# Perceiver layer on one core: where the value products and the slot work stand among the score steps, and one Newton iteration for both halves

## The reference

```
x = x + xattn(layernorm(x), ctx)      # 16 heads of 16, softmax over 4096 context rows
x = x + attn(layernorm(x))            # causal linear attention
x = x + ffn(layernorm(x))             # silu(x wg) * (x wu), then wd; 768 hidden columns

# attn: each q and k row is first divided by its norm
xn = x / jnp.maximum(jnp.linalg.norm(x, axis=-1, keepdims=True), 1e-12)
feat = jnp.exp(clip(einsum(xn, omega) * sqrt_2s - s)) / sqrt(M) ...
```

## Time and profile before

| | |
|---|---|
| median of 3 runs | 915.33 us |
| the profiled execution | 914.84 us, of which 913.1 us lie between its first and last instruction |
| granted TensorE clock, mean | 0.979 |
| TensorE busy | 844.7 us, 93% |
| ScalarE busy | 532.0 us, 58% |
| VectorE busy | 432.7 us, 47% |
| first scores of batches 0, 1, 2, 3 | 41.57, 207.38, 413.26, 619.43 us |
| end of the last values | 816.8 us |

### The profile page before, as it was taken

One profiled execution on the slowest core, in us unless ns is written; L12 is line 12 of the kernel. 1 busy time (PEld: TensorE's weight loads), 2 busy tenths in 40 slices (PEclk: granted clock), 3 DMA queues, 4 the chain that ended last, 5 costly groups with the idle time before them and its releaser, 6 DMA issues.

```text
span 913.1 us, 20640 instructions
## 1 busy us (share of the span) xinstructions
PE 844.7 (93%) x8815; PEld 573.3 (63%) x8815; DVE 432.7 (47%) x796; ACT 532.0 (58%) x578; POOL 48.3 (5%) x76
## 2 busy tenths in 40 slices
PE   6799999999999999999899999999999999978776
PEld 4566666666566666666566666666566666646555
DVE  6532235355744446535744446534744445214653
ACT  2167777676577666656577666657577666840101
POOL 1033000000000000000000000000000000000000
PEclk9899999999999999999999999999999999998799
DMA  5757564465333333336343333336334333001000
GB/s 178 236 182 246 207 206 163 147 202 174 127 140 139 139 139 133 107 135 183 128 139 139 139 140 114 116 136 191 117 139 140 139 117 116 1 24 24 1 1 15
DMA packets 58738, 120.09 MB, mean 132 GB/s; under 512 B 21521, under 2 KB 29713, under 8 KB 55121
## 3 DMA queue, kind: packets, MB, share of 16 engines
q1 hardware_dynamic: 56848, 114.31, 36.8%
q0 software_dynamic: 1792, 4.40, 1.6%
HBM read 78.84 MB, written 37.75 MB: 128 GB/s over the span
## 4 chain that ended last, share of the span: by engine, by line
PE 75%; DVE 10%; issue 6%; ACT 4%; DVEq 2%; DMA 1%; POOL 1%; SPq 0%; POOLq 0%; ACTq 0%
PE ps_o L750 23%; PE ps_s L762 16%; PE ps_pa L594 10%; PE ps_pa L555 10%; ACT probs L1026 3%; PE ps_pa L720 2%; PE ps_pa L695 2%; PE ps_pa L707 2%; PE ps_pa L686 1%; PE ps_pa L616 1%; PE ps_pa L643 1%; PE ps_pa L699 1%; DVE feat L1264 1%; DVE feat L1248 1%; DVE ss L1250 1%
## 5 line engine op out<-in xcount | busy, mean ns | idle before, releaser
L1026 ACT ACTIVATE probs<-ps_s 128x1024 f32<-128x1024 f32 x512 | 495.9, 1023 | 272.0 <-PE ps_s L762 243.1
L750 PE MATMUL ps_o<-probs,values 128*17 128x256 f32 x4096 | 258.1, 382 | 0.0
L762 PEld LDWEIGHTS ps_s<-qstack,kstack 64*128 64x128 f32 x2048 | 139.9, 185 | 116.9 <-issue 57.4
L762 PE MATMUL ps_s<-qstack,kstack 64*128 64x256 f32 x2048 | 196.8, 307 | 13.1 <-ACT probs L1026 12.2
L750 PEld LDWEIGHTS ps_o<-probs,values 128*17 128x17 f32 x4096 | 101.4, 97 | 99.4 <-issue 14.3
L1063 DVE TENSOR_SCALAR kparts<-ps_pa,b_heads 128x512 fp32r<-128x512 f32 x64 | 48.0, 751 | 123.8 <-PE ps_pa L555 123.8
L1080 DVE TENSOR_TENSOR values<-ps_pa,bv_pair 128x512 f32<-128x512 f32 x64 | 44.3, 692 | 109.6 <-PE ps_pa L594 109.3
L594 PE MATMUL ps_pa<-wv_hi,ctx_hi 128*128 128x256 f32 x256 | 78.3, 306 | 1.6 <-DVE wv_lo L1051 1.6
L594 PE MATMUL ps_pa<-wv_hi,ctx_lo 128*128 128x256 f32 x256 | 72.5, 283 | 0.0
L594 PE MATMUL ps_pa<-wv_lo,ctx_hi 128*128 128x256 f32 x256 | 72.5, 283 | 0.0
L555 PE MATMUL ps_pa<-ctx_hi,wk_hi 128*128 128x512 f32 x128 | 57.7, 451 | 4.5 <-DVE kparts L1065 2.3
(11 more groups left out here) (238 smaller groups left out, 798.1 us busy)
## 6 DMA issues: line engine op xcount, KB each, us to landing
kstack<-kscr SPq DMA_DIRECT2D x96, 512.0 KB, 5.3
...
qstack<-qscr SPq DMA_DIRECT2D x12, 256.0 KB, 3.7
...
xh<-x SPq DMA_DIRECT2D x4, 256.0 KB, 6.4
...
qstack<-ksample SPq DMA_DIRECT2D x4, 256.0 KB, 4.0
```

The source lines that it names most:

```text
L750: last = mm(ps_o[32 * j:32 * j + DH + 1, g * S:(g + 1) * S], values[par][:, i, head_of_step(g, j), :], prob[:, j * S:(j + 1) * S], start=b ...
L762: last = mm(ps_s[s % 2][:, j * S:(j + 1) * S], kstack[par][rows, u, i * P:(i + 1) * P], queries[rows, u, :], start=True, stop=True)
L1026: nc.scalar.activation(probs[n % AHEAD][:, :], ps_s[n % 2][:, :], ACT.Exp, scale=float(DH) ** -0.5).then_inc(fast["exp_done"], 1)
```

## The change

1. Quads that hold no wide stage, and all quads of batch 0, now run as: scores 0 and 1, the values of the four steps of the quad before, scores 2 and 3, and then all four slots. Quads with a wide stage keep their order. 2. `ss0` only squares and sums; `ss1` takes floor and Newton steps for both halves in one go, on 64 columns. 3. `gu0`, `gate4`, `gu5`, `gate5`, `down` and the head stages behind `ln0` move by 1 to 6 steps (so the queries `q` of the next head stand in the quad of `gu4`, ahead of its key projection, and `max0` in the quad of `gu5`); ScalarE takes a gate's tanh and copy behind the last exponential of its quad where the quad has no wide stage. 4. The warm matmuls in front of tail stages are counted anew, with 14 ahead of `A0` and 12 ahead of the wait for the verdict. 5. SyncE stores the output after the second key half instead of ahead of it.

```diff
@@ -75,18 +75,20 @@
       "norm0": 24, "norm1": 25, "qkT0": 25, "qkT1": 28,
       "feat0": 32, "feat1": 38, "A0": 42, "A1": 46, "feat2": 48, "pv0": 50, "A2": 54, "A3": 58, "pv1": 60, "feat3": 62,
       "A4": 64, "A5": 70, "pv2": 72, "A6": 74, "A7": 78, "pv3": 82, "o2T0": 84, "o2T1": 85, "y2T": 88, "wout": 89,
-      "ln2T": 94, "gu0": 97, "gate0": 98, "gu1": 99, "gate1": 100, "gu2": 101, "gate2": 104, "gu3": 105, "gate3": 108,
-      "gu4": 109, "gate4": 110, "gu5": 112, "gate5": 113, "down": 118}
+      "ln2T": 94, "gu0": 96, "gate0": 98, "gu1": 99, "gate1": 100, "gu2": 101, "gate2": 104, "gu3": 105, "gate3": 108,
+      "gu4": 109, "gate4": 112, "gu5": 115, "gate5": 116, "down": 124}
 TAIL = list(AT)
-HEAD_AT = {"ln0": 86, "ln0T": 102, "q": 106, "kbd": 110, "max0": 114, "max1": 115, "max2": 116, "max3": 117,
-           "maxT": 120}
-WARM = {"yT": 18, "ln1T": 10, "qkT0": 32, "y2T": 3, "ln2T": 10, "gu0": 3, "down": 5}
+HEAD_AT = {"ln0": 86, "ln0T": 104, "q": 108, "kbd": 110, "max0": 112, "max1": 116, "max2": 117, "max3": 120,
+           "maxT": 121}
+WARM = {"yT": 30, "ln1T": 14, "qkT0": 22, "A0": 14, "y2T": 3, "ln2T": 12, "gu0": 3, "down": 5}
+WARM_JUDGED = 12
 NORMALISED = TAIL.index("oT1") + 1
 FEATS = [f"feat{f}" for f in range(G)]
 WIDE = FEATS + [f"A{p}" for p in range(H // 2)]
 GATES = [f"gu{k}" for k in range(HB)]
 
-ACT_BEHIND = {**{n: 1 - AT[n] % 2 for n in FEATS}, **{n: 1 - AT[n] % 2 for n in GATES}}
+WIDE_QUADS = {AT[n] // QUAD for n in WIDE}
+ACT_BEHIND = {n: 1 - AT[n] % 2 if AT[n] // QUAD in WIDE_QUADS else QUAD - 1 - AT[n] % QUAD for n in FEATS + GATES}
 
 NEEDS = {"maxT": "max3", "oT0": "o", "oT1": "o", "qk1": "ln1T", "v": "ln1T", "qkT0": "norm0", "qkT1": "norm1",
          **{n: "qkT1" for n in FEATS}, **{f"A{p}": "qkT1" for p in range(H // 2)},
@@ -476,8 +478,6 @@
                         load_head(fast, b + 1, (fast["product"], fast.at("product", head_of(b), "ln0T")))
                     if q + 2 < B * NCH:
                         write_key_half(fast, q + 2, p % 2, 0)
-                    if b and p == AT["down"] // STEPS:
-                        store(fast, tail_of(b - 1), b - 1)
                     if b + 1 < B and p == HEAD_AT["q"] // STEPS:
                         write_queries(fast, head_of(b + 1))
                         stack_queries(fast, b + 1, qstacks[(b + 1) % 2])
@@ -485,6 +485,8 @@
                         shift_queries(fast, head_of(b + 1), qstacks[(b + 1) % 2])
                     if q + 2 < B * NCH:
                         write_key_half(fast, q + 2, p % 2, 1)
+                    if b and p == AT["down"] // STEPS:
+                        store(fast, tail_of(b - 1), b - 1)
             load_x(fast, B - 1, (fast["operand"], fast.at("operand", tail_of(B - 2), "down")))
             write_output(fast, tail_of(B - 1))
             regroup_output(fast, B - 1)
@@ -796,6 +798,14 @@
                     pe.wait_ge(fast["operand"], fast.at("operand", tail_of(b - 1), "o"))
                 value_product(fast, n, s, q % 2, q % NCH == 0, q % NCH == NCH - 1, q * TT + s // G)
 
+            valued = [0]
+
+            def values_up_to(n):
+
+                while valued[0] < n:
+                    fast_values(valued[0])
+                    valued[0] += 1
+
             def fast_slot(b, p, s):
 
                 q = b * NCH + p
@@ -840,25 +850,25 @@
                     pe.wait_ge(fast["k_stacked"][p % 2], (q // 2 + 1) * STACKED)
                     for s in range(0, STEPS, QUAD):
                         n = q * STEPS + s
-                        halves = s == 0 or any(name in WIDE for t in range(QUAD)
-                                               for name, _ in stages_at(b, p * STEPS + s + t))
-                        for t in (0, 1):
-                            fast_scores(b, q, s + t)
-                        for t in (0, 1):
-                            fast_slot(b, p, s + t)
-                        if halves and n:
+                        if b and (p * STEPS + s) // QUAD in WIDE_QUADS:
+                            for half in (0, 2):
+                                for t in (0, 1):
+                                    fast_scores(b, q, s + half + t)
+                                for t in (0, 1):
+                                    fast_slot(b, p, s + half + t)
+                                values_up_to(n + half)
+                        else:
                             for t in (0, 1):
-                                fast_values(n - LAG + t)
-                        for t in (2, 3):
-                            fast_scores(b, q, s + t)
-                        for t in (2, 3):
-                            fast_slot(b, p, s + t)
-                        for t in range(LAG if halves else 0, QUAD):
-                            fast_values(n - LAG + t)
-            for t in range(LAG):
-                fast_values(B * BS + t - LAG)
+                                fast_scores(b, q, s + t)
+                            values_up_to(n)
+                            for t in (2, 3):
+                                fast_scores(b, q, s + t)
+                            for t in range(QUAD):
+                                fast_slot(b, p, s + t)
+            values_up_to(B * BS)
             products(fast, TAIL[:NORMALISED], tail_of(B - 1), True)
 
+            warm(ps_p, WARM_JUDGED)
             pe.wait_ge(judged, 1)
             nc.tensor.transpose(ps_a[0:1, 0:P], den_ok[:, 0:1], ident[:, :]).then_inc(judged, 1)
             products(fast, TAIL[NORMALISED:], tail_of(B - 1), True)
@@ -1247,11 +1257,13 @@
                     sq = feat[:, 0, n, :, :].rearrange("p c s -> p (c s)")
                     v.tensor_tensor(sq, qk[:, n, :], qk[:, n, :], ALU.mult)
                     dve.drain()
-                    v.tensor_reduce(ss[:, n, :], sq.rearrange("p (h d) -> p h d", d=DH), AX.X, ALU.add)
-                    dve.drain()
-                    v.tensor_scalar(ss[:, n, :], ss[:, n, :], 1e-24, None, ALU.max)
-                    dve.drain()
-                    last = inverse_root(rnorm[:, n, :], ss[:, n, :], sq[:, 0:2 * H])
+                    last = v.tensor_reduce(ss[:, n, :], sq.rearrange("p (h d) -> p h d", d=DH), AX.X, ALU.add)
+                    if n == ST - 1:
+                        every, roots = (a[:, :, :].rearrange("p t h -> p (t h)") for a in (ss, rnorm))
+                        dve.drain()
+                        v.tensor_scalar(every, every, 1e-24, None, ALU.max)
+                        dve.drain()
+                        last = inverse_root(roots, every, sq[:, 0:ST * 2 * H])
                 elif kind == "norm":
 
                     qk3 = qk[:, n, :].rearrange("p (h d) -> p h d", d=DH)
```

## The result

The changed kernel takes 903.11 us, the median of four runs (900.96, 901.60, 904.62, 911.17), beside 915.39 for the kernel before on the same chip. The ratio is 0.9879, 95% interval 0.9836 to 0.9922. The forecast was 900.5 with a range of 894 to 908: the time lies in it, 2.6 above the forecast. A second series of six runs on another occasion gave 907.07, ratio 0.9903 (0.9867 to 0.9938).

What follows compares the result with a forecast made beforehand. TensorE, busy 93% of the span, was taken to bound the kernel with its waits. Loop gains 19.4 less costs 10.5 give 9; 914.84 - 9 - 2.6 (tail Newton) - 3.0 (tail clock) = 900.2, forecast 900.5, range 894 to 908.

Steps and rivals of the forecast that it cites:

- One sign that the prediction itself named for being wrong: Loop: a batch of 206 us that has not lost 1 to 2 us would show the prediction wrong.
- The last step of the forecast: Whole kernel: 900.2 for the profiled execution, plus 0.5 for the median of the runs, given as 900.5.
- Ordinary and first quads: Loop: ordinary quads keep 4.83 us; batch 0's chunk starts, 5.58 before, come to 4.83 too, 0.75 less each.
- the slower rival: Plain quads: ScalarE's release by values of n-4 comes 0.94 late, 0.7 lost in each of 92, 965 us; chance 0.04.
- the terms of the sum for batch 0: Batch 0: seven chunk starts gain 0.75 each; a delayed value projection costs 0.35, `maxT` and `max0` about 1.4.
- The added waits: Loop: VectorE work now in the open before `feat0`, `qk0`, `gu4`, `gu5`, `gu1` and in batch 0 costs 10.5 us.
- the claim of the gains that `oT1` only stops waiting: Loop, `oT1`: its bank waits, 0.8 us in all over three batches, go.
- Newton in the loop: Batches 1 to 3: joint Newton leaves VectorE ahead of `qk1`, so `qkT0` comes 0.7 earlier in each, 2.1 us.
- The end of batch 3: Last quad of batch 3: `down`'s 5.4 us of matmuls cover exponentials that stood in the open, about 1.6 us gained.
- Tail, Newton: Tail: joint Newton shortens a VectorE chain TensorE waits for, 2.6 us; 22 warm matmuls for 32 stay inside the wait.
- Tail, clock: Tail: fourteen warm matmuls ahead of `A0` fill 3.2 of 3.78 us idle and keep the clock at full, 3.0 us gained.
- The rule against Newton: Loop and tail: optimizing the busiest engine first would make Newton at VectorE's 47% worth nothing, the sum 4.7 us less; term kept.

Runs made afterwards that it cites:

- after_again: The changed kernel run once more with nothing altered, as the measure for the runs beside it: 907.07 us, ratio 0.990 to the kernel before.
- order_alone: Kernel before with only the new order inside quads and new places of tanh and features; old step numbers, warm matmuls and Newton: 926.43 us, ratio 1.012.

## Why the prediction was right, and where not

The time came out where it was forecast, but the sum that gave it did not hold term by term. The loop gave 5.8 of the 9 us, and 1.6 of these are the clock of the profiled execution of the kernel before. One sign that the prediction itself named for being wrong came true: batches 1 and 2 were to lose 1 to 2 us of their 206, and batch 2 takes 206.9 us, before 206.2, in `after_again` 205.6 (batch 1 204.4 both times, before 205.9). The last step of the forecast has a slip too: 900.2 and 0.5 are 900.7.

**Ordinary and first quads.** Right. 4.85 against the 4.83 forecast; no score waits for ScalarE in a plain quad, so the slower rival, a release one exponential late, did not come. Batch 0 is 5.6 shorter, of which 3.1 belong to the order; the terms of the sum for batch 0 give 3.5.

**The added waits.** Right in place and nearly in size. `feat0` 1.18 of added time in each of three batches (1.05 forecast), `qk0` 0.57 (0.6), `gu4` 0.98 (0.7), `gu5` 0.72 (0.7), `gu1` 0.38 (0.35). The next batch's first scores after batch 0 wait 1.36 for `maxT`'s transfer (1.4). `max0` in batch 0 costs 0.8 and not 0.15.

**The missed wait.** The sum has no term for the output's transfers. The step that failed is the claim of the gains that `oT1` only stops waiting, 0.8 us to the good. The quads at step 4 do lose 0.14, 0.13 and 0.48. But `oT1` also moved to the end of its quad, and its two writes leave 1.6 to 1.9 us later. That alone costs nothing, since `yT`'s turn moved by as much, as batch 1 shows. In batches 2 and 3 the second write also takes 2.2 and 1.2 us longer, and `yT` waits 1.8 and 0.8, 2.8 in all from start to start. Why it takes longer is open, so following the stages and their transfers through the new order would have found the place, but not the size.

**Newton in the loop.** At its place, steps 24 to 27, the forecast was 2.1 us and the three quads are 1.3 shorter, but not for its reason. `order_alone`, with the old Newton, has them 2.3 shorter: it is the new order that takes the wait away, and joint Newton gives 1.0 of it back. By itself it is worth 1.3 in the old order. The step that failed is the reading of the earlier trace rows: it set the new instruction stream into the old order's idle times. The two edits meet on VectorE.

**The end of batch 3.** Forecast 1.6 from `down` as cover for the last exponentials. From step 96 on the piece is 0.2 shorter while it holds two steps of values more, so on equal work it gave 1.2; with its other terms (two cuts gone, `gu1`) the sum has 1.5. ScalarE's pace did stand in the open, and stands there less now. The waits of TensorE for it from step 96 of batch 3 on, before and after:

```profile
PE ps_s L762 <- ACT probs L1026: 4.2, 9, 0.9
```

```profile
PE ps_s L764 <- ACT probs L1036: 3.3, 7, 0.9
```

So this term was right in its mechanism and somewhat too large.

Of the 9 us forecast for the loop the missed wait takes 2.8 and Newton 0.8, which leaves 5.4. The clock at the start of the kernel before adds 1.6. Measured are 5.8, so the other terms together fell 1.2 short: among them 0.6 at step 0 of batches 1 to 3 (0.77, 0.46 and 0.47 for 0.75 each), 0.4 at `feat0`, 0.6 at `gu4` and 0.4 in batch 0, against gains that the runs don't split.

**Tail, Newton.** 2.59 measured for 2.6 forecast, but as 1.69 from Newton and 0.90 from the warm count. The sentence that 22 warm matmuls for 32 are "still inside the wait" is true; that 32 would be so too, and the count therefore worth nothing, isn't.

**Tail, clock.** The profiled execution has the 3 us (`A0` to `y2T` 21.6 for 23.9, `qkT0` to `A0` 7.3 for 8.2). The size holds, and with the fourteen matmuls the clock is at full at `A0` as forecast, but the gain is not shown to be theirs: three executions with them lose as much at half clock as those without, and the medians do not differ. One step was wrong: "at that rate" 3.2 us is what they take at full clock. In a stretch at half clock they take up to 5.5, more than the wait of 3.78 that they were to fill, and then they delay `A0` themselves. The first piece of the tail and the last take 0.8 and 0.6 longer than before, the first because the output's second write takes 5.1 us and not 4.1.

**The rule against Newton.** By the prediction's reading of the Trainium skill, "Perfetto Trace Analysis", section "Identifying the Most-Contended Engine", both Newton terms would be 0. In the tail and in the old order the trace shows otherwise: VectorE at 47% is what TensorE waits for, and the gain is a wait of TensorE, the busiest engine, that got shorter. What fell is that reading, not the advice to look to the busiest engine first. In the loop of the new order joint Newton does give nothing, at the same 47%: the share of busy time doesn't tell the two cases apart.
